# Output weights split in the context stage and kept in memory; head 1's maxima in PSUM; more of the last sum on VectorE

## The reference, cut to what matters

```
x = x + xattn(layernorm(x), ctx)      # 16 query heads, 4 key/value heads of 128, 4096 + 256 keys
x = x + mamba2(layernorm(x))          # in-projection, causal conv, chunked scan, gated norm, out-projection
x = x + moe(layernorm(x))             # 32 experts of 192, top 6, and a shared expert of 384

# xattn
q, k, v = xn @ wq, xn @ wk, xn @ wv;  k_ctx, v_ctx = ctx @ wk_ctx, ctx @ wv_ctx
q, k, k_ctx = rms_norm(q), rms_norm(k), rms_norm(k_ctx);  q, k = rope(q), rope(k)
probs = softmax(q @ [k_ctx, k].T / sqrt(128) + causal mask on the last 256)
return (probs @ [v_ctx, v]) @ wo      # wo: 2048 x 512
```

## Time and profile before

| | us |
|---|---|
| median of 3 runs | 995.39 (993.46 to 995.46) |
| profiled execution | 996.27 |
| its span, first to last instruction | 994.5 |
| TensorE busy | 973.3 (98%) |
| VectorE busy | 784.6 (79%) |
| ScalarE busy | 612.4 (62%) |
| GpSimd busy | 560.9 (56%) |

### The profile page before, as it was taken

How to read it: one execution, slowest core, us unless ns; L and a number is a source line. 1 busy time by engine, 2 the same in 40 slices (tenths; PEclk the granted TensorE clock), 3 DMA queues, 4 the chain that set the end, 5 groups by cost and what they waited for, 6 DMA issues and landing times.

```text
span 994.5 us, 15791 instructions
## 1 busy us (share of the span) xinstructions
PE 973.3 (98%) x5695; PEld 857.6 (86%) x5695; DVE 784.6 (79%) x1178; ACT 612.4 (62%) x1026; POOL 560.9 (56%) x517
## 2 busy tenths in 40 slices
PE   8999999999889999999999999988999999999998
PEld 7888888889779999999999999976788988888887
DVE  6754667645988888888888898899798887777775
ACT  5443343336656777767667767774488666666663
POOL 3543444331579999999999999997001032222222
PEclk9999999999999999999999999999999999999999
DMA  8557654566202221141204032220610685555540
GB/s 289 160 184 251 212 189 128 169 227 219 105 1 87 95 75 32 44 138 46 62 1 146 36 111 109 75 95 1 235 62 1 243 310 197 189 189 188 190 159 22
DMA packets 56525, 131.10 MB, mean 132 GB/s; under 512 B 4192, under 2 KB 36352, under 8 KB 55424
## 3 DMA queue, kind: packets, MB, share of 16 engines
q1 hardware_dynamic: 56448, 130.09, 38.7%
HBM read 101.21 MB, written 28.87 MB: 131 GB/s over the span
## 4 chain that ended last, share of the span: by engine, by line
PE 90%; DVE 4%; POOL 3%; issue 2%; ACT 1%; DMA 1%; SPq 0%; DVEq 0%; POOLq 0%; ACTq 0%
PE bank L526 18%; PE bank L629 17%; PE bank L600 17%; PE bank L508 13%; PE bank L928 9%; PE bank L930 5%; POOL first_max L1918 2%; PE bank L736 1%; PE bank L535 1%; DVE first_max L1093 1%; PE bank L623 1%; PE bank L625 1%; PE bank L627 1%; DVE first_max L1085 1%; PE bank L792 1%
## 5 line engine op out<-in xcount | busy, mean ns | idle before, releaser
L600 PE MATMUL bank<-qT_hi,kT 128*128 128x256 f32 (+1 forms) x1088 | 296.0, 346 | 1.7 <-DVE first_max L1089 1.4
L1918 POOL TENSOR_TENSOR first_max<-first_max,weights 128x512 f32<-128x512 f32 x214 | 280.7, 1312 | 18.9 <-ACT weights L1627 1.0
L629 PE MATMUL bank<-weights,vN 128*128 128x256 f32 (+1 forms) x896 | 260.7, 378 | 0.0
L1623 ACT COPY weights<-bank 128x512 f32<-128x512 f32 (+1 forms) x272 | 154.8, 580 | 100.9 <-PE bank L600 61.6
L600 PEld LDWEIGHTS bank<-qT_hi,kT 128*128 128x128 f32 x1088 | 196.9, 190 | 20.7 <-issue 1.6
L1093 DVE TENSOR_TENSOR first_max<-bank,first_max 128x512 f32<-128x512 f32 x196 | 134.8, 688 | 36.7 <-ACT weights L1623 31.6
L1114 DVE TENSOR_TENSOR weights<-weights,bank 128x1024 f32<-128x1024 f32 x128 | 154.8, 1210 | 1.8 <-PE bank L656 1.8
L1627 ACT ACTIVATE weights<-weights 128x1024 f32<-128x1024 f32 x144 | 144.5, 1003 | 17.8 <-DVE weights L1114 17.7
L600 PE MATMUL bank<-qT_lo,kT 128*128 128x256 f32 (+1 forms) x544 | 153.8, 283 | 0.0
L526 PE MATMUL bank<-w_ctx_hi,ctx_hl 128*128 128x512 f32 x512 | 144.3, 393 | 1.4 <-ACT w_ctx_hi L1586 1.4
L629 PEld LDWEIGHTS bank<-weights,vN 128*128 128x128 f32 x896 | 142.7, 190 | 3.3
(11 more groups left out here) (258 smaller groups left out, 1735.0 us busy)
## 6 DMA issues: line engine op xcount, KB each, us to landing
e_raw<-in_experts SPq DMA_DIRECT2D x51, 768.0 KB, 4.4
k_spill<-k_stage SPq DMA_DIRECT2D x16, 1024.0 KB, 5.6
kT<-k_spill SPq DMA_DIRECT2D x15, 1024.0 KB, 5.3
v_spill<-v_stage SPq DMA_DIRECT2D x16, 512.0 KB, 6.7
vN<-v_spill SPq DMA_DIRECT2D x16, 512.0 KB, 3.6
ctx_raw<-in_ctx SPq DMA_DIRECT2D x15, 512.0 KB, 4.0
w_raw<-in_w_qkv SPq DMA_DIRECT2D x6, 1024.0 KB, 5.1
comb<-c_spill SPq DMA_DIRECT2D x8, 512.0 KB, 5.7
```

The source lines that it names most:

```text
L600: done = e.matmul(dst, kT[:, w, kt * P:(kt + 1) * P], qT[a][:, h, q0:L], start=m == 0, stop=m == 2)
L629: done = e.matmul(dst[:, q0:L], vN[:, kt, :], weights[:, cols], start=kt == 0, stop=kt == KTILES - 1)
L1623: e.copy(s_buf[h % 2][:, g, 0:width(g)], bank[SCORE_BANKS[s % len(SCORE_BANKS)]][:, 0:width(g)]).then_inc(taken, 1)
L1918: e.tensor_tensor(run_sum[:, :], run_sum[:, :], here, ALU.add).then_inc(summed, 1)
```

## The change

Three parts.

1. The high and low parts of wo are made in the context stage, in 32 chunks of 128 x 256 (WC = 256, NWC = 32), and kept in memory (wo_parts). For tile i SP loads chunk i into one of two buffers, ScalarE casts it into the single buffer wo_main at the end of its step i, GpSimd subtracts in its step i+1, and SP stores both parts. The loads of wo before the last head become loads of its low part, and four loads of 1 MB fetch the high part as head 14's weights are used up. The casts and subtractions in the last head go, and the products with wo begin three groups later (WO_MAIN 243 to 246, WO_REST 249 to 250).
2. Head 1's running maximum is kept in PSUM bank 5. Head 0's fold is two maxima. Head 1's maxima are turned and spread one group later.
3. OWN_SUMS goes from 6 to 2. GpSimd makes the low part of the weights of a SPLITS group one group earlier.

```diff
-TURN_AT, REDUCE_AT, SPREAD_AT = (5, 4, 2), (2, 5, 3), (7, 6, 3)
+TURN_AT, REDUCE_AT, SPREAD_AT = (5, 5, 4, 2), (2, 5, 5, 3), (7, 7, 6, 3)
-OWN_SUMS = 6
+OWN_SUMS = 2
-WO_CASTS, WO_MAIN, WO_LOWS, WO_REST = 241, 243, 246, 249
+WO_MAIN, WO_REST = 246, 250
+WC = DM // 2
+NWC = NH * DM // WC
...
             # TensorE
             def project_main(tt, i):
-                pe.wait_ge(wo_hi_done, i + 1)
+                pe.wait_ge(wo_hi_in[h // 4], 16 * NKV + 16)
...
             # VectorE
+            def maxima_of(h):
+                return bank[VALUE_BANKS[1]] if h == 1 else run_max
...
-                    e.tensor_tensor(run_max[:, :], here[:, :], run_max[:, :], ALU.max).then_inc(maxed, 1)
+                    e.tensor_tensor(top[:, :], here[:, :], top[:, :], ALU.max).then_inc(maxed, 1)
...
+                if h == 0:
+                    e.tensor_tensor(first_max[:, 0, :], first_max[:, 0, :], first_max[:, 1, :], ALU.max).then_inc(maxed, 1)
+                    dve.wait_ge(maxed, plan.folded[0] - 1)
+                    e.tensor_tensor(both_max[:, :], first_max[:, 0, 0:L], first_max[:, 0, L:2 * L], ALU.max).then_inc(maxed, 1)
+                    return
...
-            def rest_of_wo(i):
-                h = WO_ORDER[i]
-                dve.wait_ge(wo_hi_done, i + 1)
-                e.tensor_tensor(wo_lo[:, h, :], wo_sb[:, h, :], wo_hi[:, h, :], ALU.subtract).then_inc(wo_lo_done, 1)
...
             # ScalarE, at the end of step i of the context stage
+            def main_of_wo(c):
+                act.wait_ge(wo_chunk_in, 16 * (c + 1))
+                act.wait_ge(wo_parts_out, 32 * c)
+                e.copy(wo_main[:, :], wo_chunk[c % 2][:, :]).then_inc(wo_hi_done, 1)
...
+                main_of_wo(i)
...
             # GpSimd, in step i behind split_ctx(i + 1)
+            def rest_of_wo(c):
+                pool.wait_ge(wo_hi_done, c + 1)
+                e.tensor_tensor(wo_chunk[c % 2][:, :].bitcast(F32R), wo_chunk[c % 2][:, :], wo_main[:, :], ALU.subtract).then_inc(wo_lo_done, 1)
...
+                if i:
+                    rest_of_wo(i - 1)
...
             for n in range(NH * NG):
-                if n % NG in SPLITS:
-                    rest_of_weights(n)
+                if (n + 1) % NG in SPLITS:
+                    rest_of_weights(n + 1)
                 add_weights(n)
...
             # SyncE
+            def load_wo(c):
+                h, cols = wo_columns(c)
+                if c >= 2:
+                    sp.wait_ge(wo_parts_out, 32 * (c - 1))
+                e.dma_start(wo_chunk[c % 2][:, :], t["wo"][:, h, cols]).then_inc(wo_chunk_in, 16)
+
+            def spill_wo(c):
+                h, cols = wo_columns(c)
+                sp.wait_ge(wo_hi_done, c + 1)
+                e.dma_start(wo_parts[0][:, h, cols], wo_main[:, :].bitcast(F32)).then_inc(wo_parts_out, 16)
+                sp.wait_ge(wo_lo_done, c + 1)
+                e.dma_start(wo_parts[1][:, h, cols], wo_chunk[c % 2][:, :]).then_inc(wo_parts_out, 16)
...
+                load_wo(i)
+                if i:
+                    spill_wo(i - 1)
...
+            for j in range(NH // 4):
+                sp.wait_ge(pv, NG * (H15 - 1) + 4 * j + 4)
+                sp.wait_ge(summed, summed_at(H15 - 1, 4 * j + 3))
+                e.dma_start(wo_hi[:, 4 * j:4 * j + 4, :].bitcast(F32), wo_parts[0][:, 4 * j:4 * j + 4]).then_inc(wo_hi_in[j], 16)
```

## The result

| | before | after |
|---|---|---|
| median of 4 executions, us | 994.97 (993.46 to 995.46) | 1012.18 (1008.57 to 1015.81) |
| profiled execution, us | 996.27 | 1008.57 |
| its span, us | 994.5 | 1006.7 |

The change makes the kernel slower: the ratio is 1.0176, 95% interval 1.0132 to 1.0219. Forecast were 1001.6 us and a range up to 1010; the direction was right, the size was not. The profiled execution of the kernel after was the quickest of its four.

What follows compares the result with a forecast made beforehand. TensorE, busy in every stretch, was taken to bound the kernel through its waits and the clock behind them. 20.1 - 8.9 - 5.0 = +6.2 on the profiled 996.3 gave 1002.5, median 1001.6 us; range 989 to 1010.

Steps and rivals of the forecast that it cites:

- Start: Context stage: the cast of chunk 0 waits for its load and delays the first projection weights' split, +4.5 us, bounds 1 to 6.
- Tile 27: Context stage: chunk transfers land behind two megabytes of keys, stalling project(29) 6.1 us, plus 1.7 for clock: +7.8 us.
- Four weight tiles: Context stage, tiles 4, 8, 12, 16, behind projection weight loads: TensorE stalls 1.7 us at each, +6.8 us, bounds 0 to 12.
- The other tiles have 2 us or more to spare: Context stage: the remaining tiles cost nothing, since ScalarE splits a whole tile ahead.
- Last step: End of the context stage: ScalarE's first copy of scores stands behind the cast of chunk 31, +1.0 us, bounds 0 and 3.
- transfers finish in the order of issue: SP's queue in the context stage: small transfers land behind those issued earlier, 0.35 us per 128 KB in a busy queue.
- The first two heads: Heads 0 and 1: two-maxima fold, PSUM maxima and earlier low parts shorten VectorE's work and clear waits, -8.9 us.
- The last head: Last head: wo's subtractions and casts go, GpSimd finishes sooner, waits for wo_lo, wo_hi and pT go: -5.0 us.
- Rival (3): Context stage: every stall slows the clock too and writes land later, 1009 us; chance 0.12.
- (1): Context stage: the handshake is hidden because small transfers don't queue behind large ones, 982.5 us; chance 0.13.
- (2): Context stage: only start, tile 27 and the end stall, the four weight tiles just in time, 994.8 us; chance 0.11.
- (4): First two heads: the PSUM destination for head 1's maxima doesn't pay, 1008.5 us; chance 0.08.

Runs made afterwards that it cites:

- cast_mid: The changed kernel with ScalarE's cast of chunk i-1 moved from the end of its step to the middle of step i: 987.06 us, ratio 0.9922 to the kernel before.
- parts_first: The changed kernel with SP issuing the chunk's load and the stores ahead of the next context load: 1001.66 us, ratio 1.0067 to the kernel before.
- mid_low_late: cast_mid with GpSimd's low parts of the weights made at their own group again, not one sooner: 991.15 us, ratio 0.9963 to the kernel before.
- mid_sbuf_max: cast_mid with head 1's running maximum in SBUF again, fold and later turn kept: 995.75 us, ratio 1.0007 to the kernel before.
- again: The changed kernel unaltered, timed and traced a second time (the second trace): 1013.24 us, ratio 1.0178 to the kernel before.
- mid_spread: cast_mid with head group 0's four key loads one to a tile, at tiles 26 to 29: 987.22 us, ratio 0.9929 to the kernel before.
- mid_one_fold: cast_mid with head 0's fold as one reduction again in place of two maxima: 989.95 us, ratio 0.9951 to the kernel before.

## Why the prediction was wrong in size and right in direction

The median came 10.6 us above the forecast (1012.2 for 1001.6). About 6 of it stand in the profiled execution (1008.6 for 1002.5): +6.8 in the context stage, +0.4 in the first two heads, -1.2 in the last. The other 4.5 lie between that execution and the median. Two steps failed: that the tiles without a weight load have 2 us to spare, with the weight tiles priced one by one at 1.7 us, and that the clock falls only once in the context stage.

**What bounds the kernel** was right: in every kernel here the time moved with TensorE's waits and the clock behind them, and the context stage's added work cost nothing by itself (cast_mid).

**The context stage, +20.1 forecast, +26.9 in the trace.** The mechanism was the one named, step by step: ScalarE's cast waits for the stores and holds up the split behind it. The sizes:
- Start, +4.5: 4.7. Tile 27, +7.8: 6.9, with the clock; the wait is 5.4 where 6.1 was worked out.
- Four weight tiles, +6.8: 10.9. Three gave 2.0, 2.0 and 2.6. The one ahead of turn(5) gave 4.3, for its wait was 2.5 and its clock fell, at a place where the forecast had left the clock alone.
- "The other tiles have 2 us or more to spare": this step failed. Project(4) stalled and lost 2.1 us. The forecast took each tile by itself, from the trace before, as if the cast before it were in time. But the handshake is a loop: low part, SP's context load, stores, landing, cast, split, next low part. Once the start has made it late it doesn't catch up before TensorE has stalled at 59.4. parts_first shortens the loop at SP and the delay at turn(5), start not counted, falls from 6.4 to 2.5 us.
- Last step, +1.0: 1.9.

The case built on a small transfer overtaking a large one didn't come, for the cast waits for both stores, and the second of them, the low part's, was late: issued behind a context load alone it landed after 4.3 us, behind a set of weights as well after 7.3, and behind the weights without the context load (parts_first) after 5.1. But the prediction's "transfers finish in the order of issue" is not right either. These were issued at 49.72 (the context load), 50.57 (the high part) and 51.05 (the low part):

```profile
ctx_raw<-in_ctx SPq DMA_DIRECT2D x1, 512.0 KB, 7.5
wo_parts<-wo_main SPq DMA_DIRECT2D x1, 128.0 KB, 5.5
wo_parts<-wo_chunk SPq DMA_DIRECT2D x1, 128.0 KB, 7.2
```

The high part landed at 56.1, 1.1 us ahead of the load of 57.2 that was issued before it; the low part landed last, at 58.3. The Trainium skill ("DMA: Bandwidth & Descriptors", section on queues, rings and completion order) says that completion is not first-in first-out for one issuing engine. Here the trace agrees, by a microsecond and for the first store alone, which is no gain to the cast.

**The first two heads, -8.9:** -8.5, with VectorE's gain from PSUM at 6.3 us for the 6.4 forecast, and the cleared waits and clock. Two parts of the reasoning were off. GpSimd's earlier low parts were not what gained there (mid_low_late). And 1.9 us for the two masked pieces isn't "the same ratio": 0.688 to 1.245 on their 1.39 and 1.24 us gives 1.2. They did gain 1.9 (mid_sbuf_max), so that term came out right by luck.

**The last head, -5.0:** -6.2, inside its bounds. The low part one group sooner, which the forecast took into account in the first two heads alone, pays here.

**The median.** The forecast took it to lie 0.9 us below the profiled execution, as before. It lies 3.6 above. That is the other failed step: the forecast put one slow stretch into the context stage; the trace has two, and the second trace five. Rival (3), every stall slows the clock too, had 1009 us and 12%. It was the nearest of the cases, but not for what it counts: its clock comes to 7.3 us (1.7 behind tile 27, 1.6 behind the start, 4 behind the four tiles), the first trace lost 3.1 and the second 8.4, and the stall of project(4) isn't in it.

**The other rivals.** (1) is out by the 79 us of the cast's waits, of which 15.4 reach TensorE; (2) by the waits at turns 5, 9, 13 and 17; (4) by mid_sbuf_max. (1)'s number, 982.5, is near what the change comes to once the cast is moved (986 to 987), for what it gave up was this wait.

**What stays open.** Why a wait of some 2 us is followed by low clock in one place and not in another: in again the clock fell behind a wait of 1.8 us ahead of turn(9) and stayed up behind one of 1.8 ahead of turn(13); ahead of turn(17) it stayed up behind 2.0 us in the first trace and fell behind 2.1 in the second. Why the low clock behind the wait at the key loads costs 1.7 us in some kernels and 3.4 in others. Why mid_spread's executions differ by 4.6 us. The start's +4.7 was never taken apart from the rest: it went together with the tiles in cast_mid.

## What to carry to other kernels

Work that is free as busy time can be dear by its place in a queue: before adding an instruction that waits for a transfer, look at what stands behind it on that engine, and put it where the next instruction isn't wanted for as long as the transfer takes to land. Follow such a wait around until it closes; if it is a loop, the slack of one tile is no measure, the length of the loop against the period is. And when many short waits of the bounding engine are added, price the clock behind each, and expect the executions to lie further apart (7.2 us here, 2.0 before).

## What was not expected of the hardware

A stretch of low clock cost 1.6 to 1.7 us in each of the five of the second trace, whether the wait ahead of it was 1.8 us or 5.5, and the same kernel had two in one trace and five in the other. At the key loads it cost 1.7 us in cast_mid and 3.4 in mid_one_fold, parts_first and mid_sbuf_max, behind waits of 3.6, 4.3, 5.5 and 3.8 us. A PSUM destination, of which no row of the kernel before spoke, costs VectorE 0.693 us for a maximum of 128x512 while GpSimd adds weights in SBUF, no more than one in SBUF with GpSimd at rest (0.69 at 256.9 us of the kernel before), while the same maximum with both operands and result in SBUF averages 1.0 over the head and 1.39 in place of 0.43 for its masked piece of 256 columns.
